# Causal attention with the queries and keys of a group loaded in two halves, and the written orders of all engines in a group made anew

## The reference

```python
x = L0_attn_x
xn = _layernorm(x, axis=-1)
s = _L0_attn_ref(xn, ...)          # 16 heads, causal, softmax over up to 2048 keys
g = _silu(_L0_ffn_ref(xn, ...))    # 2 layers, window of 128
x = x + s * g
```

```python
scores = jnp.einsum('bhqd,bhkd->bhqk', qc, k) * scale
scores = jnp.where(causal_mask[None, None], -jnp.inf, scores)
p = jax.nn.softmax(scores - m, axis=-1)
oc = jnp.einsum('bhqk,bhkd->bhqd', p, v)
```

## Time and profile before

| | us |
|---|---|
| median of 3 runs | 4688.48 |
| lowest and highest run | 4687.99, 4694.49 |
| the profiled execution | 4683.54 |
| its span, first to last instruction | 4681.6 |

### The profile page before, as it was taken

One profiled execution on the slowest core, in us unless ns is written; L12 is line 12 of the kernel. 1 busy time (PEld: TensorE's weight loads), 2 busy tenths in 40 slices (PEclk: granted clock), 3 DMA queues, 4 the chain that ended last, 5 costly groups with the idle time before them and its releaser, 6 DMA issues. The chain is left out here.

```text
span 4681.6 us, 91449 instructions
## 1 busy us (share of the span) xinstructions
PE 4380.3 (94%) x31896; PEld 2944.6 (63%) x31896; DVE 3570.9 (76%) x7576; ACT 2978.6 (64%) x6873; POOL 1393.5 (30%) x1940
## 2 busy tenths in 40 slices
PE   8589999999999999689999999999999999999976
PEld 7433443344434433378788788887887878878866
DVE  7498878888877887377777777777777777777746
ACT  2157777777777777456576666665666666666642
POOL 3112222222222222333333333333333333333300
PEclk9779999999999999899999999999999999999999
DMA  8833334433333341200000000010100000000008
GB/s 296 250 52 57 57 81 74 82 58 61 58 57 54 68 72 44 80 14 24 19 24 15 27 16 19 24 37 33 66 24 19 24 19 24 15 28 15 19 14 287
DMA packets 187392, 270.02 MB, mean 58 GB/s; under 512 B 75984, under 2 KB 127056, under 8 KB 180048
## 3 DMA queue, kind: packets, MB, share of 16 engines
q1 hardware_dynamic: 186960, 264.39, 22.6%
HBM read 158.38 MB, written 105.38 MB: 56 GB/s over the span
## 5 line engine op out<-in xcount | busy, mean ns | idle before, releaser
L723 ACT ACTIVATE a_pt<-a_ring 128x512 f32<-128x512 f32 (+3 forms) x2560 | 1180.5, 544 | 443.7 <-PE a_ring L847 426.8
L774 DVE TENSOR_REDUCE a_mx<-a_ring 128x2 f32<-128x1024 f32 (+3 forms) x1079 | 1117.1, 1064 | 252.1 <-PE a_ring L867 122.8
L860 PE MATMUL a_ring<-a_ks,a_qs 48*128 48x512 f32 (+3 forms) x2560 | 558.2, 432 | 89.2 <-DMA a_ks<-qk_d 55.4
L847 PE MATMUL a_ring<-a_qs,a_ks 49*128 49x512 f32 (+3 forms) x2560 | 563.5, 447 | 58.5 <-ACT a_pt L723 29.2
L1139 POOL TENSOR_TENSOR l_rn<-l_ssm,l_half 128x8 f32<-128x8 f32 x256 | 419.2, 1637 | 650.6 <-DVE l_ssm L1392 650.6
L884 PE MATMUL a_ot<-a_pt,a_vt 128*32 128x512 f32 (+3 forms) x5120 | 606.0, 553 | 1.8 <-ACT a_os L729 1.3
L1238 ACT ACTIVATE l_pr<-l_pr,l_negm 128x256 f32<-128x256 f32 (+1 forms) x1024 | 503.1, 497 | 115.7 <-DVE l_negm L1444 115.2
L847 PEld LDWEIGHTS a_ring<-a_qs,a_ks 49*128 49x128 f32 x2560 | 249.4, 188 | 465.7 <-ACT a_pt L723 268.4
L664 POOL TENSOR_TENSOR a_gate<-a_gate 128x1 f32<-128x1 f32 x512 | 98.8, 193 | 1286.8 <-ACT a_pt L723 1276.9
L860 PEld LDWEIGHTS a_ring<-a_ks,a_qs 48*128 48x128 f32 x2560 | 259.5, 192 | 345.0 <-ACT a_pt L723 170.2
L1146 POOL TENSOR_TENSOR l_work<-l_work,l_rot 128x512 f32<-128x512 f32 x256 | 340.0, 1334 | 393.6 <-DVE l_work L1400 393.6
(11 more groups left out here) (167 smaller groups left out, 9095.5 us busy)
## 6 DMA issues: line engine op xcount, KB each, us to landing
qk_d<-p_parts SPq DMA_DIRECT2D x16, 2048.0 KB, 9.7
a_qs<-qk_d SPq DMA_DIRECT2D x96, 256.0 KB, 8.3
a_ks<-qk_d SPq DMA_DIRECT2D x96, 256.0 KB, 18.2
l_rot<-rot_s SPq DMA_DIRECT2D x32, 512.0 KB, 3.9
x_d<-l_dx SPq DMA_DIRECT2D x32, 512.0 KB, 2.7
l_xt<-x_d SPq DMA_DIRECT2D x24, 513.0 KB, 4.9
p_x_in<-x SPq DMA_DIRECT2D x16, 512.0 KB, 8.4
x_d<-p_xt SPq DMA_DIRECT2D x16, 512.0 KB, 4.5
```

The costliest lines, as they stand in the source:

```text
L723: act.activation(pt[:, (g * STEPS + s) % NPT, 2 * piece + f, q0:CHUNK], bank("step", g, k, f)[:, q0:CHUNK], ACT.Exp).then_inc(exp_done.sem, 1)
L774: r = dve.tensor_reduce(mx[:, pr, :, t, kc], ring[:, banks[0]:banks[1] + 1, 0:w], AX.X, ALU.max)
L847: pe.matmul(bank("step", g, k, f)[:, q0:CHUNK], ks[rows, g % NSLOT, piece, kt * P:(kt + 1) * P], qs[rows, g % NSLOT, piece, c * CHUNK + q0 ...
L860: mm = pe.matmul(bank("unit", G, n, f)[:, 0:w], qs[rows, v, pr, q0:q0 + P], ks[rows, v, pr, kc * CHUNK:kc * CHUNK + w], start=True, stop=k ...
```

## The change

Queries and keys of a group are fetched in two halves by columns, 0 to 1023 and 1024 to 2047, each half for all of `qs` and `ks`: twice as many transfers, each of half the size, in the same queue. Each slot has two semaphores. TensorE waits for the first half at unit 0, and for the second at the first unit of chunk 2, which is unit 24.

The orders in a group are written anew for all engines. Work and its amount are the same on each. TensorE is one unit further ahead at a group's start (units 0 to 47 come ahead of the first group).

```diff
-        loaded = [tally(f"loaded{u}", 16 * 4 * NSTACK) for u in range(NSLOT)]
+        loaded = [[tally(f"loaded{u}{h}", 16 * 4 * NSTACK) for h in range(2)] for u in range(NSLOT)]
...
         def tensor_order(do):
-            do("step", 0); do("unit", 47); do("weigh", -4); do("step", 1); do("unit", 48); do("step", 2)
+            do("step", 0); do("unit", 48); do("weigh", -4); do("step", 1); do("unit", 49); do("weigh", -3)
...
                 sp.wait_ge(pv_done.sem, pv_done.at(G - NSLOT))
-                for dst, pick, o in ((qs, STACK_Q, 0), (ks, STACK_K, NGROUP)):
-                    for j, s in enumerate(pick):
-                        for f in range(2):
-                            row = f * HALF + j * A_HD
-                            sp.dma_start(dst[row:row + A_HD, v].bitcast(F32), parts_v[s, f, :, hg + o, :, b])\
-                              .then_inc(loaded[v].sem, 16)
+                for h in range(2):
+                    cols = slice(h * SEQ // 2, (h + 1) * SEQ // 2)
+                    for dst, pick, o in ((qs, STACK_Q, 0), (ks, STACK_K, NGROUP)):
+                        for j, s in enumerate(pick):
+                            for f in range(2):
+                                row = f * HALF + j * A_HD
+                                sp.dma_start(dst[row:row + A_HD, v, :, cols].bitcast(F32),
+                                             parts_v[s, f, :, hg + o, :, b, cols]).then_inc(loaded[v][h].sem, 16)
...
             def around(do):
-                do("row_out", 1); do("row_out", 2); do("load", 1); do("out", -1); do("out", 0)
-                do("item_out", -1); do("row_out", 3); do("row_out", 4); do("out", 1)
-                do("keep", 0); do("item_in", 1); do("out", 2)
+                do("row_out", 1); do("row_out", 2); do("out", -2); do("load", 1); do("out", -1); do("out", 0)
+                do("item_out", -1); do("row_out", 3); do("out", 1); do("row_out", 4); do("keep", 0)
+                do("item_in", 1)
...
-                do("widen", 1)
                 do("split", 0)
-                for n in range(49, 80):
+                for n in range(49, 76):
+                    do("step", n)
+                do("widen", 1)
+                for n in range(76, 80):
                     do("step", n)
...
-                if n == 0:
-                    pe.wait_ge(loaded[v].sem, loaded[v].per * (G // NSLOT + 1))
+                if n in (0, units.index((CPB // 2, 0, 0, 0))):
+                    half_ = loaded[v][c // (CPB // 2)]
+                    pe.wait_ge(half_.sem, half_.per * (G // NSLOT + 1))
```

More of the change, by code:

```diff
@@ new lines, in tensor_order @@
+            do("step", 2); do("unit", 50); do("weigh", -2); do("weigh", -1); do("row_out", 2); do("unit", 51)
+            do("step", 3); do("unit", 52); do("step", 4); do("step", 5); do("weigh", 0); do("step", 6)
+            do("step", 7); do("unit", 53); do("step", 8); do("unit", 54); do("weigh", 1); do("step", 9)
+            do("unit", 55); do("step", 10); do("unit", 56); do("weigh", 2); do("step", 11); do("unit", 57)
+            do("step", 12); do("out", -1); do("step", 13); do("unit", 58); do("weigh", 3); do("unit", 59)
@@ new lines, in tensor_order @@
+            do("step", 36); do("unit", 85); do("unit", 86); do("step", 37); do("out", 1); do("step", 38)
+            do("unit", 87); do("step", 39); do("row_out", 3); do("weigh", 16); do("step", 40); do("unit", 88)
+            do("step", 41); do("weigh", 17); do("unit", 89); do("step", 42); do("unit", 90); do("step", 43)
+            do("unit", 91); do("step", 44); do("unit", 92); do("step", 45); do("unit", 93); do("weigh", 18)
+            do("step", 46); do("fold", 0); do("step", 47); do("unit", 94); do("row_out", 4); do("step", 48)
@@ L497, in attend @@
+            do("unit", 119); do("step", 71); do("unit", 120); do("weigh", 32); do("unit", 121); do("step", 72)
+            do("unit", 122); do("step", 73); do("unit", 123); do("weigh", 33); do("step", 74); do("unit", 124)
+            do("step", 75); do("unit", 125); do("weigh", 34); do("unit", 126); do("row_out", 5); do("step", 76)
+            do("step", 77); do("weigh", 35); do("step", 78); do("step", 79); do("unit", 127)
         held = [None] * NB
@@ L802, in around @@
                 do("out", -3)
[L803 removed]
+                for n in range(7, 15):
                     do("unit", n)
                 do("fold", -1)
[L806 removed]
+                for n in range(15, 27):
                     do("unit", n)
```

78 lines of the change are left out of this document (31 added, 47 removed).

## The result

| | before | after |
|---|---|---|
| median, us | 4691.48 (4 runs) | 4645.85 (4 runs) |
| lowest and highest run | 4687.99, 4708.82 | 4642.85, 4647.18 |
| the profiled execution | 4683.54 | 4647.18 |
| its span | 4681.6 | 4645.2 |

The ratio of after to before is 0.9895, with an interval from 0.9869 to 0.992. The change makes the kernel 1.05% faster. Against the profiled execution, 28 us were forecast and 36.4 came.

A forecast was written before the change was run, and what follows sets the result against it. No engine alone was taken as the attention stage's bound: TensorE, VectorE and ScalarE pass PSUM banks around. Start 12.4, keys' wait 11, fold 3.7 and VectorE's reductions 1 made 28 us off 4688.48: 4660.5 us, range 4638 to 4684.

The forecast's parts named there:

- The start: Attention stage's first score matmul: waits only for the first half of keys and queries, 12.4 us earlier (bounds 0 to 14).
- Rival (b): At the stage's start the halves land no sooner, transfers paying for their number; steady gain stays: 4673 us, chance 0.06.
- the rule that spoke for it: Skill's rule on loads: merge small transfers, about 2 us fixed cost each; twelve more would add 24 us if paid in turn.
- The keys' wait: TensorE's waits for the keys' transfer in the steady groups vanish: 11 us, between 6.5 (matmuls) and 15.6 (weight loads).
- rival (c): Attention groups: shorter wait and denser stretches also keep the clock up, saving the fold's whole wait too: 4644 us, chance 0.10.
- The load's place: In SyncE's queue the load follows row_out 2, which moves up, so it starts some nine steps, 11 us, earlier in a group.
- The fold's bank: In the four w1 groups, unit 95 and its reduction move behind the add, shortening TensorE's bank wait: 3.7 us (0 to 8.5).
- The rest of the order: New sequence where no old wait is named, all attention groups: taken at 0, give or take 1 us a group, 15 us.
- (a): Only the stage's start gains; at the load's and fold's places a VectorE or ScalarE hole takes over: 4676 us, chance 0.12.
- (d): Slower: the clock falls in each group at the new run of four, steps 62 to 65: 4720 us, chance 0.08.
- (e): The change doesn't do what it says, for instance unit 24 or 104 waits for the second half: 4688 us, chance 0.04.
- GpSimd's masks: At a group's head TensorE might wait for a mask behind v's widening, at most 1.2 us a group; costed at nothing.

The follow-up runs named there:

- e2: Kernel after, with the load as before (twelve whole transfers, one wait at unit 0) and the new orders kept; 4658.24 us, ratio 0.9935.
- e1: Kernel before, with only the load by halves and two semaphores a slot, all orders old; 4652.18 us, ratio 0.9921.
- e4: Kernel after, with one of the fold's eleven matmuls and weight loads, ten result columns left out; 4626.85 us in one run.
- e7: Kernel after, with the load in quarters and one added matmul behind each of the first group's units 8 to 47; 4645.43 us, ratio 0.9885.
- e9: Kernel after, load in quarters, 24 matmuls back to back ahead of unit 0 and one more behind each of units 8 to 47; 4648.5 us in one run.
- e12: Kernel after, with the load in four quarters (48 transfers of 64 KB, a semaphore each), timed a second time; 4634.01 us, ratio 0.9887.
- e3: Kernel before, with 24 half transfers but unit 0 waiting for both halves, orders old; 4657.53 us in one run.
- e6: Kernel after, with one added 512-column matmul behind each of the first group's units 8 to 47; 4661.06 us, ratio 0.9913.

## Why the prediction was right, and where it was off

**The start: right.** Forecast 12.4 us, measured 13.5 at the first exponential, and 13.9 from first issue to unit 0. The half landed a little sooner than the queries of before did. That unit 24 would not wait was right as well. Rival (b), no sooner landing, fell with the 210.65; the rule that spoke for it doesn't hold for these sizes.

**What the start gave back: not foreseen.** "VectorE's 42.75 busy us are the same behind the earlier start, so the gain isn't given back" was true only as far as step 0. In the first group 5.6 us came back. Part of it is the start: the clock rose at 280.3 in after and at 281.2 in before, though the steps began 13.5 us sooner. Part is a second stretch: in after the clock fell again at 317.8, 61 us into the group, for 6.8 us, which at 0.41 are 2.8. All ten profiles with the new order have this second stretch, 58 to 62 us in, e2 included, and none of the four with the old order has one there. e1, with the same start in the old order, rose at 266 and lost nothing (101.4 us). Both the early start and the new order are in all kernels that rose only 21 to 24 us into the group (after, e4 to e7, e9 to e12); e2, with the new order alone, didn't. That it takes the new order together with a load in parts is what the runs show; why, they don't. In after the next group's load runs there (DMA share 0.73, against 0.01 in before), but so does it in e2 (0.53), where the clock rose after 14.

**The keys' wait: gone as forecast, sized too high, and the clock was no term of the sum.** Taken at 11 us, the wait was worth 7 to 9 by the table, and in the three groups where it stands alone just what the matmuls waited, which over all groups is the lower bound, 6.5. But in the old order e1 and e3 took 19 and 26 us off the fourteen groups by the load alone, since they also had 24 and 41 us less at the lower clock. The sum put the clock at nothing, and it stood only as rival (c) with 0.10. The prediction also read the earlier trace rows as three of ten groups without a fold in which the old run of four took the clock down; the trace has four (the 15th too), and its second profile six.

**The load's place: the size was off.** I expected the load 11 us earlier in the group. In after it starts 6.4 us behind the group's first exponential (1077.12 against 1070.73), in before 14.0 (1111.58 against 1097.56), so 7.6 us earlier. Row_out 2's transpose stands 4.0 us into the group instead of 12.3: the nine steps at the head of a group took 8.3 us, not nine times the mean step, and the store that now goes ahead takes 0.4. These are the rows of after:

```profile
1070.73 1.09 ACT L727 ACTIVATE a_pt<-a_ring 128x512 f32<-128x512 f32 x2 [0.20 <-PE a_ring L851]
```

```profile
1077.12 2.83 SPq L571 DMA_DIRECT2D a_qs<-qk_d  x6
...
1089.05 13.49 SPq L583 DMA_DIRECT2D o_d<-a_otok  x2
```

It made no difference, since one or two would have done (e3). The two stores behind the load took SyncE 13.49 us and held nobody up.

**The fold's bank: right.** Forecast 3.7 us, measured 3.4 (8.5 to 5.1), with 1.28 us in each group where about 1.2 was named.

**The rest of the order: wrong, but within its 15 us.** Taken at 0, it is worth 0.9 us a group, 12.6 in the fourteen, of which VectorE's reductions are a part (one was forecast). Against e1 it is mostly given back: 5.8 us in the first group, and 4.7 in the last of the fourteen (103.8 us against 99.1), where the clock fell for 10.2 us at step 44 and for 3.4 at step 64. What the new orders add to the halves is 3 us of the stage, less than the runs can tell: the ratios of e1 (0.9893 to 0.995) and after (0.9869 to 0.992, 0.9897 to 0.9926) overlap.

**The rivals.** (a), only the start gains, fell: 28.7 us came from the fourteen groups. (c), the clock stays up too, named 4644, close to the time, but for other reasons in part: the fold's bank still costs 5.1 us of 8.5, and the gain includes the order's pace. (d), slower, was right in its place and wrong in its price: in after the clock falls at step 64 in six of the fourteen groups, for 3.4 us each (in three of the four with a fold that is 87 us into the group, in the others 81 and 85). That is 1.4 us each, about 8 in all, and not 60. The other place that the prediction named, the narrow run at steps 42 to 45, took the clock down too, at step 44 in the last of the fourteen. The fourteen have twelve stretches now and had eight, where "as many as now" was forecast, but they are shorter, 61 us together instead of 75. (e) fell with the start.

**GpSimd's masks** were the close call it was taken for: weight loads wait for them at the head of fourteen groups, no matmul does there, and the time doesn't show it.

**The sum, as measured** (the keys' wait is what the other prices leave): start 13.5, keys' wait 7.0, clock 5.7, fold's bank 3.4, order 12.6, last group 1.6, less 5.6 in the first group and 1.8 behind the stage, is 36.4 us. The forecast's 28 were 8.4 short: the clock and the order weren't in it, and neither was what the first group gave back. The wait's price and the first group were set too high for the gain, the clock and the order too low; that these offset each other in part, and the time stayed in the range, is luck.

## What to carry to other kernels

Give the first transfer of a stage the size that its first consumer needs, and a semaphore of its own; go on in this way until the issues themselves are the limit, for smaller pieces cost nothing here down to 64 KB. Give TensorE's clock a term of its own in the sum, and take its price from groups that differ only in one low stretch (here 1.4 us for 3.4). Before a wait is blamed for a fall of the clock, list the groups that have either: here they were not the same groups. Before an order is written anew by hand, try the transfer change alone: here it gave 35 of the stage's 38 us.

## What was not expected of the hardware

- The first group's 3 MB landed in 27.3 to 27.9 us as twelve transfers of 256 KB (three profiles), in 24.3 to 26.2 as 24 of 128 KB (six), and in 24.3 to 25.2 as 48 of 64 KB (five), at 0.45 us an issue.
- TensorE can be busy without a gap by the profile and remain at a granted clock of 0.50: 31 us in e6. Twenty-four matmuls of 128 rows and 512 columns, back to back, raised it after 5.5 us (e9), and it fell again 1.5 us into the units, behind 2.9 us without work.
- Eleven matmuls of one column, 2.62 us of work, cost a group 5.8 us, 3.4 of them by the clock (e4).
- Groups of the same kernel and the same order differ between two profiles by the number of low stretches alone: 75 and 85 us in the fourteen groups of before, 61 and 72 in those of after.
